# Attention scores in four PSUM banks instead of six, with one row maximum per two pairs of tokens

## The chip, the cores and the metric

The kernel runs on the 8 cores of one Trainium2 chip. Every core runs the same program on its own 2048 of the 16384 tokens, and no data passes between cores. The metric is the device time in microseconds of the slowest core, so lower is better.

## The reference

One layer in the form `x + attention(xn) + ffn(xn)`, where `xn` is the layer norm of `x` (1 x 16384 x 4096).

```python
q = einsum('bse,edh->bsdh', xn, Wq) + bq          # D = 128, 32 heads
k, v = (the same with 8 heads), then repeated 4 times
scores = einsum('bsdh,bseh->bsde', q, k) / sqrt(D)  # 128 x 128 for each token
attn = softmax(scores, axis=-1)
out = einsum('bsde,bseh->bsdh', attn, v)
...
base = einsum('bsi,oi->bso', xn, W)                # W from 4-bit weights, scale and zero
lora = einsum(einsum(xn, lora_A), lora_B) * 2
return x + out + base + lora
```

What is unusual is the attention. It doesn't run over positions: for each token by itself the 128 channels of q meet the 128 channels of k, with the heads as the contracted dimension. So there are 2048 score matrices of 128 x 128 on each core, each contracted over 8 head groups (the kernel has summed the four q heads that share a k head) or, with one more row for the maximum, over 9.

## The kernel before, in words

A core works through its 2048 tokens in 4 chunks of 512. A chunk has four stages, and the program writes them one behind the other on every engine, so each engine's queue has the same order:

1. The layer norm and its transposes into `xnT` (lines 285 to 380).
2. The projections for q, k and v (`qkv_t`, the matmuls of line 460) with weights that stream through the ring `wring`, and the small LoRA product (line 535).
3. The attention, in 16 batches of 32 tokens. A batch has 16 pairs of tokens. This is the stage that the change touches.
4. The FFN in 8 blocks of 512 columns (line 880), whose 4-bit weights VectorE (lines 830 and 833) and ScalarE (line 852) unpack just ahead of the matmuls.

A batch of the attention goes through these steps, each with its line:

- `_shf_half` (line 578): 16 small DMAs, 8 issued by SyncE and 8 by ScalarE, bring 32 tokens of q and k into `qg_sh` and `k_sh`, with heads on partitions. They wait until the B matmuls of the batch before are done.
- `att_A` (line 609): TensorE makes the scores of each pair (two matmuls of 128 columns, so 256 columns of f32 in PSUM), only so that a maximum can be taken.
- `att_rm` (line 626): VectorE takes the maximum of each row of each of the two score matrices, into two columns of `Mb`. There is one instruction per pair, 16 in a batch.
- `att_mt`, `att_mte`, `att_md` (lines 637, 648, 660): the maxima are transposed on TensorE, copied to SBUF and moved by one DMA into row 8 of `qg_sh`.
- `att_BAV` (lines 683 and 700): TensorE makes the scores again, transposed and with the maximum subtracted by the ninth contracted row (B), ScalarE takes the exponential (line 725), and TensorE multiplies the result with v (AV). On TensorE the order is B of pair 0, B of pair 1, AV of pair 0, B of pair 2, AV of pair 1, and so on.
- `att_rc` and `att_og` (lines 735 and 751): VectorE divides by the sum of the row.

Where scores lie in PSUM is said by `att_pp_aps`. A PSUM bank holds 512 columns of f32, hence two pairs. Six banks are used in turn: `pf0`, `pf1` and the four banks of `pAB`. Pair number `pp` takes bank `pp % 6`, and each second time round the other half of the bank. The waits go by bank and not by half:

```python
if pin >= 6:
    e.wait_ge(sem["rm"].h, rm_prev + pin - 5)
elif b > 0 or c > 0:
    e.wait_ge(sem["exp"].h, exp_prev + pin - 5)
```

In words, the A matmuls of pair `pin` wait until the maximum of pair `pin - 6` is taken. In the same way B of a pair waits for the exponential of the pair 6 before it. The stages around also use these banks: `pf0`, `pf1` and the first two banks of `pAB` hold the four results of 128 tokens in the projections and in the FFN.

Of the kernel before, what the change touches and what calls it, by code (L numbers as in the profile page):

```python
# [66 lines left out]
def build_program():  # L67
# [20 lines left out]
    with ExitStack() as ctx:  # L88
# [18 lines left out]
        Mb = sb("Mb", [128, 2 * 32], BF16)  # L107
# [31 lines left out]
        pf0 = psum("pf0", [128, 512], F32)  # L139
        pf1 = psum("pf1", [128, 512], F32)  # L140
        pAB = psum("pAB", [128, 2048], F32)
# [6 lines left out]
        sem = {n: S(nc, ctx, "s_" + n) for n in names}  # L148
# [127 lines left out]
        for c in range(min(NCH, KCHUNKS)):  # L276
# [273 lines left out]
            evq_ce = sem["evq"].v  # L550
            e7_vchan = sem["e7"].v

            def att_pp_aps(pp):
                sl = pp % 12
                bk = sl % 6
                hf = sl // 6
                if bk == 0:
                    t, off = pf0, hf * 256
                elif bk == 1:
                    t, off = pf1, hf * 256  # L560
                else:
                    t, off = pAB, (bk - 2) * 512 + hf * 256
                dsts = [t[:, off + j * 128: off + (j + 1) * 128] for j in range(2)]
                src = t.ap().rearrange("p (k x) -> p k x", x=128)[:, off // 128: off // 128 + 2, :]
                return dsts, src

            for b in (range(min(NBAT, KBATCH)) if KPHASE >= 3 else []):
                mblk = b // 4

# [19 lines left out]
                def att_A(e, c=c, b=b, rm_cb=rm_cb, exp_cb=exp_cb, evq_ce=evq_ce):  # L589
                    if KSTAGE < 1:  # L590
                        return
                    e.wait_ge(sem["shf"].h, sem["shf"].v)
                    if b == 0:
                        e.wait_ge(sem["evq"].h, evq_ce)
                        e.wait_ge(sem["evl"].h, sem["evl"].v)
                        e.wait_ge(sem["exp"].h, sem["exp"].v)
                    exp_prev = sem["exp"].v
                    rm_prev = sem["rm"].v
                    for pin in range(16):
                        pp = b * 16 + pin  # L600
                        dsts, _ = att_pp_aps(pp)
                        if pin >= 6:
                            e.wait_ge(sem["rm"].h, rm_prev + pin - 5)
                        elif b > 0 or c > 0:
                            e.wait_ge(sem["exp"].h, exp_prev + pin - 5)
                        last = None
                        for j in range(2):
                            slot = 2 * pin + j
                            last = e.matmul(dsts[j],  # L609
                                            qg_sh[0:8, slot * 128:(slot + 1) * 128],  # L610
                                            k_sh[0:8, slot * 128:(slot + 1) * 128],
                                            start=True, stop=True,
                                            skip_group_check=(j == 1))
                        sem["A"].inc(last)
                blk.tensor(att_A)

                def att_rm(e, b=b):
                    if KSTAGE < 2:
                        return
                    if sem["mdma"].v >= 32:  # L620
                        e.wait_ge(sem["mdma"].h, sem["mdma"].v - 16)
                    for pin in range(16):
                        e.wait_ge(sem["A"].h, sem["A"].v - 16 + pin + 1)
                        _, src = att_pp_aps(b * 16 + pin)
                        dstm = Mb[:, (b % 2) * 32 + 2 * pin: (b % 2) * 32 + 2 * pin + 2]
                        i = e.reduce_max(dstm, src, axis=AX.X, negate=True)  # L626
                        sem["rm"].inc(i)
                blk.vector(att_rm)

                t7b = sem["t7"].v  # L630
# [33 lines left out]
                def att_BAV(e, b=b, exp_cb=exp_cb, c=c, e7_vchan=e7_vchan):  # L664
                    if KSTAGE < 5:
                        return
                    e.wait_ge(sem["mdma"].h, sem["mdma"].v)
                    if b == 0:
                        e.wait_ge(sem["e7"].h, e7_vchan)
                    exp_start = sem["exp"].v  # L670
                    t0 = b * 32

                    def emit_B(pin):
                        pp = b * 16 + pin
                        dsts, _ = att_pp_aps(pp)
                        e.wait_ge(sem["rm"].h, sem["rm"].v - 16 + pin + 1)
                        need_ex = exp_start + pin - 5
                        if need_ex > 0:
                            e.wait_ge(sem["exp"].h, need_ex)
                        last = None  # L680
                        for j in range(2):
                            slot = 2 * pin + j
                            last = e.matmul(dsts[j],  # L683
                                            k_sh[0:9, slot * 128:(slot + 1) * 128],
                                            qg_sh[0:9, slot * 128:(slot + 1) * 128],
                                            start=True, stop=True,
                                            skip_group_check=True)
                        sem["B"].inc(last)

                    def emit_AV(pin):  # L690
                        if KSTAGE < 7:
                            return
                        e.wait_ge(sem["exp"].h, exp_start + pin + 1)
                        for j in range(2):
                            spos = 2 * pin + j
                            tok = t0 + spos
                            eslot = 2 * ((b * 16 + pin) % 4) + j
                            if spos == 0:
                                e.wait_ge(sem["ogs"].h, sem["ogs"].v)
                            ins = e.matmul(pV[:, spos * 9:spos * 9 + 9],  # L700
                                           Et[:, eslot * 128:(eslot + 1) * 128],
                                           v_chan[:, tok:tok + 8 * 512 + 1:512],
                                           start=(spos == 0), stop=(spos == 31))
                            sem["AV"].inc(ins)

                    for pin in range(16):
                        emit_B(pin)
                        if pin >= 1:
                            emit_AV(pin - 1)
                    emit_AV(15)  # L710
                blk.tensor(att_BAV)

                def att_exp(e, b=b, av_cb=av_cb):
                    if KSTAGE < 6:
                        return
                    for pin in range(16):
                        pp = b * 16 + pin
                        e.wait_ge(sem["B"].h, sem["B"].v - 16 + pin + 1)
                        need_av = av_cb + 2 * pp - 6
                        if need_av > 0:  # L720
                            e.wait_ge(sem["AV"].h, need_av)
                        _, src = att_pp_aps(pp)
                        eslot = 2 * (pp % 4)
                        dst = Et.ap().rearrange("p (s d) -> p s d", d=128)[:, eslot:eslot + 2, :]
                        i2 = e.activation(dst, src, AF.Exp, scale=INVSQ)  # L725
                        sem["exp"].inc(i2)
                blk.scalar(att_exp)

                def att_rc(e, b=b, ogs_cb=ogs_cb):
# [53 lines left out]
            for nb in (range(FNB) if KPHASE >= 4 else []):  # L783
# [80 lines left out]
                for half in range(2):  # L864
                    for m in range(MT):
                        def ffn_tmh(e, c=c, nb=nb, half=half, m=m, u0=u0,
                                    dqc0=dqc0, evq_ce=evq_ce, fui=fui):
                            if nb == 0 and half == 0 and m == 0:
                                e.wait_ge(sem["evq"].h, evq_ce)
                                e.wait_ge(sem["exp"].h, sem["exp"].v)  # L870
                            if half == 0 and fui >= 1:
                                e.wait_ge(sem["vt2"].h, 2 * (4 * (fui - 1) + m) + 1)
# [147 lines left out]
```

## Time and profile before

| what | value |
|---|---|
| time, median of 2 runs | 6877.63 us (6769.39 and 6985.87) |
| profiled execution, its own time | 6769.94 us |
| its span, slowest core (core 2) | 6768.2 us |
| spans of the 8 cores | 6730.1 to 6768.2 us |
| busy: TensorE matmul, VectorE, ScalarE | 3745.6, 1350.8, 1230.0 us |

The span runs from the first to the last instruction of the slowest core; the profiled execution's own time is 1.7 us longer than its span. Engines are PE (TensorE matmul), PEld (its weight load), DVE (VectorE), ACT (ScalarE), POOL (GpSimd) and SP (SyncE). A "q" behind a name is the engine's queue that issues DMAs. L609 is line 609 of the kernel. The share of busy time is a mean over four very different stages, so what follows reads the attention stage by itself.

### The profile page before, as it was taken

The numbers are of one execution on the slowest core, as the hardware profiler recorded it, in microseconds if no ns is written. First come the engines' busy times: TensorE is split into PE (matmuls) and PEld (weight loads), VectorE is DVE, ScalarE is ACT, GpSimd is POOL, SyncE is SP. The second block draws the span as 40 slices with busy tenths as digits, with TensorE's granted clock in tenths as the row PEclk, the third lists the DMA queues.
The fourth block names the chain that finished last, engine by engine and source line by source line (L and its number), as shares of the span: only waits on it lengthen the run. The fifth ranks groups of instructions, "written<-read, shape, count | busy, mean of one in ns | idle before, by whom it ended". The sixth has DMA issues, their size and how long they took to land.

```text
span 6768.2 us, 53961 instructions; the slowest of 8 cores (6730.1 to 6768.2 us)
## 1 busy us (share of the span) xinstructions
PE 3745.6 (55%) x17600; PEld 1620.1 (24%) x17600; DVE 1350.8 (20%) x2259; ACT 1230.0 (18%) x1664; POOL 272.6 (4%) x518
## 2 busy tenths in 40 slices
PE   0566644556266664456526666446562666544655
PEld 0222222212122222222112222222221222222222
DVE  3000122233300012222330001222323000222233
ACT  2000022222300002222230001222223000123222
POOL 0000000000000000000000000000000000000000
PEclk9878755667578875567658886556775888655767
DMA  2566400222212210023222221002222222100232
GB/s 72 136 169 163 126 6 6 74 103 95 91 68 88 91 56 6 6 79 111 97 80 75 87 88 49 6 6 103 92 97 75 87 87 88 37 6 11 105 107 80
DMA packets 146717, 508.58 MB, mean 75 GB/s; under 512 B 68100, under 2 KB 68308, under 8 KB 97302
## 3 DMA queue, kind: packets, MB, share of 16 engines
q0 software_dynamic: 62128, 378.23, 17.6%
q1 hardware_dynamic: 52840, 72.35, 3.1%
q10 hardware_dynamic: 31488, 54.56, 2.2%
q8 instruction: 159, 2.61, 0.2%
q14 instruction: 102, 0.84, 0.0%
HBM read 458.34 MB, written 84.03 MB: 80 GB/s over the span
## 4 chain that ended last, share of the span: by engine, by line
PE 44%; DMA 19%; DVE 13%; ACT 11%; issue 9%; ACTq 4%; DVEq 0%; SPq 0%; POOLq 0%; POOL 0%
PE pf L460 13%; PE pAB L460 9%; PE pAB L880 6%; PE pf L880 6%; ACT wring L852 5%; DMA wring<-wbq 4%; ACTq L578 4%; DVE Mb L626 3%; ACT Et L725 3%; PE pV L700 2%; DMA wring<-wq 2%; DMA qtb<-qt 2%; PE pAB L683 2%; DVE dqs L833 2%; DMA qg_sh<-Mt_s 2%
## 5 line engine op out<-in xcount | busy, mean ns | idle before, releaser
L460 PE MATMUL pf<-wring,xnT 128*128 128x512 bf16 x3072 | 873.8, 455 | 714.5 <-DMA wring<-wbq 326.3
L880 PE MATMUL pf<-wring,xnT 128*128 128x512 bf16 x2048 | 714.0, 511 | 507.6 <-ACT wring L852 507.6
L725 ACT ACT_TABLE_LOAD x64 | 82.1, 1283 | 3383.6 <-PE pf L683 2742.9
L460 PE MATMUL pAB<-wring,xnT 128*128 128x512 bf16 x3072 | 678.7, 379 | 0.0
L460 PEld LDWEIGHTS pf<-wring,xnT 128*128 128x128 bf16 x3072 | 339.7, 113 | 1246.8 <-issue 1019.6
L852 ACT ACTIVATE wring<-dqs 128x2048 bf16<-128x2048 int32 x256 | 488.8, 1909 | 585.5 <-DVE dqs L830 261.6
L880 PEld LDWEIGHTS pf<-wring,xnT 128*128 128x128 bf16 x2048 | 228.3, 119 | 987.6 <-issue 900.4
L880 PE MATMUL pAB<-wring,xnT 128*128 128x512 bf16 x2048 | 452.5, 379 | 0.0
L460 PEld LDWEIGHTS pAB<-wring,xnT 128*128 128x128 bf16 x3072 | 300.6, 98 | 362.4
L700 PE MATMUL pV<-v_chan,Et 128*128 128x9 bf16 x2048 | 216.6, 180 | 221.8 <-ACT Et L725 215.2
L609 PE MATMUL pAB<-k_sh,qg_sh 8*128 8x128 bf16 x1360 | 202.6, 290 | 225.7 <-DMA k_sh<-k_rm 224.5
L366 PE MATMUL pT<-identb,xns 128*128 128x128 bf16 x512 | 64.7, 306 | 455.8 <-ACT xns L349 410.1
L683 PE MATMUL pAB<-qg_sh,k_sh 9*128 9x128 bf16 x1360 | 246.1, 285 | 121.4 <-DMA qg_sh<-Mt_s 108.3
L493 DVE CAST qg_rm<-pf 128x512 bf16<-128x512 f32 x16 | 10.3, 686 | 1513.5 <-PE pf L471 1513.5
L725 ACT ACTIVATE Et<-pAB 128x256 bf16<-128x256 f32 x680 | 256.2, 384 | 175.4 <-PE pV L700 139.4
L626 DVE TENSOR_REDUCE Mb<-pAB 128x2 bf16<-128x256 f32 x680 | 241.1, 413 | 200.3 <-PE pAB L609 200.3
L880 PEld LDWEIGHTS pAB<-wring,xnT 128*128 128x128 bf16 x2048 | 200.5, 98 | 241.5
L830 DVE TENSOR_SCALAR dqs<-qtb 128x2048 int32<-128x2048 int32 x128 | 156.8, 1225 | 465.2 <-ACT wring L852 246.5
L700 PEld LDWEIGHTS pV<-v_chan,Et 128*128 128x128 bf16 x2048 | 137.2, 106 | 434.5 <-issue 434.4
L833 DVE TENSOR_SCALAR dqs<-qtb 128x2048 int32<-128x2048 int32 x128 | 157.1, 1227 | 315.1 <-ACT wring L852 253.8
L806 POOL DMA_DIRECT2D qtb<-qt x128 | 68.5, 536 | 3608.0 <-DVE dqs L833 3582.2
L735 DVE RECIPROCAL rz<-pV 128x32 f32<-128x32 f32 x64 | 22.9, 357 | 942.7 <-PE pV L700 942.7
(101 smaller groups left out, 2246.3 us busy)
## 6 DMA issues: line engine op xcount, KB each, us to landing
qtb<-qt POOLq DMA_DIRECT2D x128, 1024.0 KB, 5.1
wring<-wbq POOLq DMA_DIRECT2D x96, 1024.0 KB, 6.6
wring<-wq POOLq DMA_DIRECT2D x32, 1024.0 KB, 9.0
xt<-xin SPq DMA_DIRECT2D x16, 2048.0 KB, 8.0
wbq<-wring ACTq DMA_DIRECT2D x32, 1024.0 KB, 5.0
xr<-xin POOLq DMA_DIRECT2D x128, 256.0 KB, 5.9
out<-cmbU SPq DMA_DIRECT2D x128, 256.0 KB, 2.0
wring<-wbk POOLq DMA_DIRECT2D x24, 1024.0 KB, 6.6
```

Source lines behind the costliest of these rows:

```text
L460: ins = e.matmul(banks[m], xnT_ap(k, m), wring[:, slot * 512:(slot + 1) * 512], start=(jj == 0 and half == 0 and k == half * 16), stop=False)
L578: e.dma_start(out=dstv, in_=srcv).then_inc(sem["shf"].h, 16)
L609: last = e.matmul(dsts[j], qg_sh[0:8, slot * 128:(slot + 1) * 128], k_sh[0:8, slot * 128:(slot + 1) * 128], start=True, stop=True, skip_gr ...
L626: i = e.reduce_max(dstm, src, axis=AX.X, negate=True)
L683: last = e.matmul(dsts[j], k_sh[0:9, slot * 128:(slot + 1) * 128], qg_sh[0:9, slot * 128:(slot + 1) * 128], start=True, stop=True, skip_gr ...
L700: ins = e.matmul(pV[:, spos * 9:spos * 9 + 9], Et[:, eslot * 128:(eslot + 1) * 128], v_chan[:, tok:tok + 8 * 512 + 1:512], start=(spos == ...
L725: i2 = e.activation(dst, src, AF.Exp, scale=INVSQ)
L806: e.dma_start(out=qtb[:, (h % 2) * 2048:(h % 2 + 1) * 2048], in_=src).then_inc(sem["qtl"].h, 16)
L830: i = e.tensor_scalar(dqs[:], srcq, 4, None, ALU.logical_shift_right)
L833: i = e.tensor_scalar(dqs[:], srcq, 15, None, ALU.bitwise_and)
L852: i = e.activation(wring[:, s0 * 512:(s0 + 4) * 512], dqs[:], AF.Identity)
L880: ins = e.matmul(banks4[m], xnT_ap(k, m), wring[:, slot * 512:(slot + 1) * 512], start=(k == 0), stop=(k == 31))
```

## The change

Four things are done.

- The ring of score banks has four banks instead of six, all in `pAB`. Pair `pp` takes bank `pp % 4`, and each second time round the other half. A of a pair from the fifth on waits for the maximum that covers the pair 4 before it, and B waits for the exponential of the pair 4 before it.
- VectorE takes the maxima of two pairs with one instruction, which reads 256 columns in each of two neighbouring banks and writes four columns of `Mb`. There are 8 such instructions in a batch, and each waits for A of both its pairs.
- The waits on the maxima (`rm`) are counted in these new units, so two pairs of A wait for the same count.
- In the FFN the wait for all exponentials (`exp`) stands ahead of the third group of matmuls (`m == 2`, which writes `pAB`) and not ahead of the first (`m == 0`, which writes `pf0`).

```diff
                     for pin in range(16):
                         pp = b * 16 + pin
-                        dsts, _ = att_pp_aps(pp)
-                        if pin >= 6:
-                            e.wait_ge(sem["rm"].h, rm_prev + pin - 5)
+                        sl = pp % 8
+                        bcol = (sl % 4) * 512 + (sl // 4) * 256
+                        if pin >= 4:
+                            e.wait_ge(sem["rm"].h, rm_prev + (pin - 4) // 2 + 1)
                         elif b > 0 or c > 0:
-                            e.wait_ge(sem["exp"].h, exp_prev + pin - 5)
+                            e.wait_ge(sem["exp"].h, exp_prev + pin - 3)
                         last = None
                         for j in range(2):
                             slot = 2 * pin + j
-                            last = e.matmul(dsts[j],
+                            last = e.matmul(pAB[:, bcol + j * 128:bcol + (j + 1) * 128],
...
-                    for pin in range(16):
-                        e.wait_ge(sem["A"].h, sem["A"].v - 16 + pin + 1)
-                        _, src = att_pp_aps(b * 16 + pin)
-                        dstm = Mb[:, (b % 2) * 32 + 2 * pin: (b % 2) * 32 + 2 * pin + 2]
+                    for pj in range(8):
+                        e.wait_ge(sem["A"].h, sem["A"].v - 16 + 2 * pj + 2)
+                        sl = (b * 16 + 2 * pj) % 8
+                        a0 = ((sl % 4) * 512 + (sl // 4) * 256) // 256
+                        src = pAB.ap().rearrange("p (a j x) -> p a j x", j=2, x=128)[:, a0:a0 + 3:2, :, :]
+                        dstm = Mb[:, (b % 2) * 32 + 4 * pj: (b % 2) * 32 + 4 * pj + 4].rearrange(
+                            "p (a j) -> p a j", j=2)
                         i = e.reduce_max(dstm, src, axis=AX.X, negate=True)
                         sem["rm"].inc(i)
...
-                        e.wait_ge(sem["rm"].h, sem["rm"].v - 16 + pin + 1)
-                        need_ex = exp_start + pin - 5
+                        sl = pp % 8
+                        bcol = (sl % 4) * 512 + (sl // 4) * 256
+                        e.wait_ge(sem["rm"].h, sem["rm"].v - 8 + pin // 2 + 1)
+                        need_ex = exp_start + pin - 3
...
                             if nb == 0 and half == 0 and m == 0:
                                 e.wait_ge(sem["evq"].h, evq_ce)
+                            if nb == 0 and half == 0 and m == 2:
                                 e.wait_ge(sem["exp"].h, sem["exp"].v)
```

On TensorE, the A matmuls of the first batch stood like this before. A row is a line of the kernel, the operation, what it writes and reads, its size, the semaphores that it waits for, and how many such instructions follow one another. `s_rm` counts the maxima:

```order
L609 MATMUL pf<-k_sh,qg_sh 128x128 [waits s_shf,s_evq,s_evl,s_exp]
L609 MATMUL pf<-k_sh,qg_sh 128x128 x3
L609 MATMUL pAB<-k_sh,qg_sh 128x128 x8
L609 MATMUL pf<-k_sh,qg_sh 128x128 [waits s_rm]
L609 MATMUL pf<-k_sh,qg_sh 128x128
L609 MATMUL pf<-k_sh,qg_sh 128x128 [waits s_rm]
```

and they stand like this now:

```order
L596 MATMUL pAB<-k_sh,qg_sh 128x128 [waits s_shf,s_evq,s_evl,s_exp]
L596 MATMUL pAB<-k_sh,qg_sh 128x128 x7
L596 MATMUL pAB<-k_sh,qg_sh 128x128 [waits s_rm]
L596 MATMUL pAB<-k_sh,qg_sh 128x128
L596 MATMUL pAB<-k_sh,qg_sh 128x128 [waits s_rm]
```

The first wait on a maximum stood behind 12 matmuls (six pairs) and stands behind 8 (four pairs).

On VectorE, the maxima of a later batch and what follows them stood like this before:

```order
L626 TENSOR_REDUCE Mb<-pAB 128x2 [waits s_A] x2
L626 TENSOR_REDUCE Mb<-pf 128x2 [waits s_A] x2
L626 TENSOR_REDUCE Mb<-pAB 128x2 [waits s_A] x4
L626 TENSOR_REDUCE Mb<-pf 128x2 [waits s_A] x2
L626 TENSOR_REDUCE Mb<-pAB 128x2 [waits s_A] x4
L626 TENSOR_REDUCE Mb<-pf 128x2 [waits s_A] x2
L651 UNCONDITIONAL_BRANCH
L648 COPY Mt_s<-pT 32x128 [waits s_t7]
```

and they stand like this now:

```order
L616 TENSOR_REDUCE Mb<-pAB 128x4 [waits s_A] x8
L641 UNCONDITIONAL_BRANCH
L638 COPY Mt_s<-pT 32x128 [waits s_t7]
L731 UNCONDITIONAL_BRANCH
L728 RECIPROCAL rz<-pV 128x32 [waits s_AV]
```

Sixteen instructions of two columns each have become eight of four columns.

On TensorE, at the end of a chunk's attention, the last AV matmuls, the transposes of the result and the first FFN matmuls stood like this before:

```order
L700 MATMUL pV<-v_chan,Et 128x9 [waits s_exp]
L700 MATMUL pV<-v_chan,Et 128x9
L770 UNCONDITIONAL_BRANCH
L766 MATMUL pT<-identb,og 128x128 [waits s_ogs,s_e7]
L766 MATMUL pT<-identb,og 128x128 x7
L889 UNCONDITIONAL_BRANCH
L880 MATMUL pf<-wring,xnT 128x512 [waits s_evq,s_exp,s_dqc]
```

and they stand like this now:

```order
L691 MATMUL pV<-v_chan,Et 128x9 [waits s_exp]
L691 MATMUL pV<-v_chan,Et 128x9
L763 UNCONDITIONAL_BRANCH
L759 MATMUL pT<-identb,og 128x128 [waits s_ogs,s_e7]
L759 MATMUL pT<-identb,og 128x128 x7
L883 UNCONDITIONAL_BRANCH
L874 MATMUL pf<-wring,xnT 128x512 [waits s_evq,s_dqc]
```

The wait on `s_exp` has left the first FFN matmul; the matmuls ahead of it, which wait on `s_exp` themselves, stand where they stood.

## Rows read from the trace of the kernel before

**Rows 1.** The page: the span, and busy tenths in 40 equal slices.
```profile
span 6768.2 us, 53961 instructions; the slowest of 8 cores (6730.1 to 6768.2 us)
...
PE   0566644556266664456526666446562666544655
...
DVE  3000122233300012222330001222323000222233
...
PEclk9878755667578875567658886556775888655767
DMA  2566400222212210023222221002222222100232
```

**Rows 2.** Busy time by stretch: the attention stages of the four chunks.
```profile
core 2: us, PE busy (x) PEld busy (x) DVE busy (x) ACT busy (x) POOL busy (x), PEclk, DMA share, GB/s
808.00:1238.00 430.00, 210.83 (x1569) 113.03 (x1569) 103.43 (x305) 115.99 (x270) 0.00 (x0) 0.50 0.03 6
2474.00:2904.00 430.00, 209.27 (x1553) 111.91 (x1550) 103.42 (x305) 114.67 (x266) 0.00 (x0) 0.50 0.03 6
4139.00:4569.00 430.00, 209.46 (x1546) 111.75 (x1544) 104.09 (x306) 112.53 (x261) 0.00 (x0) 0.51 0.03 6
5804.00:6244.00 440.00, 219.79 (x1605) 116.28 (x1603) 104.14 (x307) 116.84 (x272) 0.00 (x0) 0.51 0.03 6
```

**Rows 3.** Chain that ended last, one batch: start us, us, what.
```profile
862.70 1.01 PE pAB L609 x8
863.71 0.43 PE pf L609 x4
864.14 0.65 PE pAB L609 x6
864.84 0.32 DVE Mb L626
...
867.16 1.42 DVE Mb L626 x4
869.59 1.76 DMA qg_sh<-Mt_s
```

**Rows 4.** Timeline of VectorE in the same batch: start us, us, instructions merged.
```profile
863.18 1.42 DVE L626 TENSOR_REDUCE Mb<-pAB 128x2 bf16<-128x256 f32 x4 [5.44 <-PE pAB L609]
...
866.50 0.74 DVE L626 TENSOR_REDUCE Mb<-pf 128x2 bf16<-128x256 f32 x2
867.16 1.40 DVE L626 TENSOR_REDUCE Mb<-pAB 128x2 bf16<-128x256 f32 x4
```

**Rows 5.** Timeline of TensorE in the same batch.
```profile
862.70 1.01 PE L609 MATMUL pAB<-k_sh,qg_sh 8*128 8x128 bf16 x8 [5.97 <-DMA k_sh<-k_rm]
863.51 0.63 PE L609 MATMUL pf<-k_sh,qg_sh 8*128 8x128 bf16 x4
863.93 1.17 PE L609 MATMUL pAB<-k_sh,qg_sh 8*128 8x128 bf16 x8
865.07 0.70 PE L609 MATMUL pf<-k_sh,qg_sh 8*128 8x128 bf16 x4
868.82 0.26 PE L637 MATMUL pT<-identb,Mb 128*32 128x128 bf16 x1 [1.73 <-DVE Mb L626]
```

**Rows 6.** Timeline of VectorE, 864.6 to 864.8 us: the batch's fifth maximum.
```profile
864.51 0.41 DVE L626 TENSOR_REDUCE Mb<-pf 128x2 bf16<-128x256 f32 x1
```

**Rows 7.** Lines 609 and 493, one instruction: min/median/max ns.
```profile
L609 PE MATMUL pAB<-k_sh,qg_sh x1360: 211/306/309, 808.3 to 6226.7; 8*128 8x128 bf16 x195
...
L493 DVE CAST qg_rm<-pAB x16: 678/680/682, 388.4 to 5611.0; 128x512 bf16<-128x512 f32 x16
```

**Rows 8.** Timeline of VectorE, 380 to 390 us: reads of 512 PSUM columns.
```profile
387.21 1.29 DVE L493 CAST qg_rm<-pf 128x512 bf16<-128x512 f32 x2 [193.84 <-PE pf L471]
388.42 1.28 DVE L493 CAST qg_rm<-pAB 128x512 bf16<-128x512 f32 x2
```

**Rows 9.** Groups by line: exponentials, maxima, and two sizes of reduction: busy us, mean ns.
```profile
L725 ACT ACTIVATE Et<-pAB 128x256 bf16<-128x256 f32 x680 | 256.2, 384 | 175.4 <-PE pV L700 139.4 <-PE pAB L683 8.6
...
L626 DVE TENSOR_REDUCE Mb<-pAB 128x2 bf16<-128x256 f32 x680 | 241.1, 413 | 200.3 <-PE pAB L609 200.3
...
L309 DVE TENSOR_REDUCE ss<-xt 128x1 f32<-128x4096 f32 x16 | 70.7, 4419 | 40.9 <-DMA xt<-xin 40.7
...
L312 DVE TENSOR_REDUCE ss<-sq 128x1 f32<-128x2048 f32 x16 | 36.4, 2276 | 0.0
```

**Rows 10.** Timeline of ScalarE in the same batch: the exponentials.
```profile
874.88 0.86 ACT L725 ACTIVATE Et<-pAB 128x256 bf16<-128x256 f32 x2 [0.72 <-PE pV L700]
876.16 0.86 ACT L725 ACTIVATE Et<-pf 128x256 bf16<-128x256 f32 x2 [0.42 <-PE pV L700]
```

**Rows 11.** Timeline of TensorE, end of the first chunk's attention.
```profile
1239.22 0.20 PE L700 MATMUL pV<-v_chan,Et 128*128 128x9 bf16 x2 [0.28 <-ACT Et L725]
1240.75 1.01 PE L766 MATMUL pT<-identb,og 128*128 128x128 bf16 x8 [1.32 <-DVE og L751]
1247.30 1.87 PE L880 MATMUL pf<-wring,xnT 128*128 128x512 bf16 x4 [5.54 <-ACT wring L852]
```

More of the change, by code:

```diff
@@ L551, in build_program @@
             e7_vchan = sem["e7"].v
[L553 to L565, printed above, removed]
             for b in (range(min(NBAT, KBATCH)) if KPHASE >= 3 else []):
@@ L674, in emit_B @@
                         pp = b * 16 + pin
-                        dsts, _ = att_pp_aps(pp)
-                        e.wait_ge(sem["rm"].h, sem["rm"].v - 16 + pin + 1)
-                        need_ex = exp_start + pin - 5
+                        sl = pp % 8
+                        bcol = (sl % 4) * 512 + (sl // 4) * 256
+                        e.wait_ge(sem["rm"].h, sem["rm"].v - 8 + pin // 2 + 1)
+                        need_ex = exp_start + pin - 3
                         if need_ex > 0:
@@ L682, in emit_B @@
                             slot = 2 * pin + j
-                            last = e.matmul(dsts[j],
+                            last = e.matmul(pAB[:, bcol + j * 128:bcol + (j + 1) * 128],
                                             k_sh[0:9, slot * 128:(slot + 1) * 128],
@@ L721, in att_exp @@
                             e.wait_ge(sem["AV"].h, need_av)
-                        _, src = att_pp_aps(pp)
+                        sl = pp % 8
+                        bk = ((sl % 4) * 512 + (sl // 4) * 256) // 128
+                        src = pAB.ap().rearrange("p (k x) -> p k x", x=128)[:, bk:bk + 2, :]
                         eslot = 2 * (pp % 4)
```

## The prediction

> **What bounds the kernel now.** I read the page first, for the shape of the run: four times over, a stretch with DMA near zero and TensorE's granted clock at 5 to 6 tenths [rows 1]. These are the attention stages. Busy time by stretch then says what each is: about 430 us long, with TensorE busy for 210, VectorE for 104 and ScalarE for 115 us [rows 2]. No engine is near full, so the stage is bound by a chain and not by throughput. The granted clock is 0.50 to 0.51, the lower of the two levels (1.2 GHz). The chain of one batch shows where the change acts [rows 3]. From the first A matmul at 862.70 us it runs through A matmuls and then through maxima on VectorE, and ends with four maxima in a row at 867.16 + 1.42 = 868.58 us. Only then come the transpose on TensorE at 868.82 us, which waited for the maxima [rows 5], and the DMA of the maxima [rows 3]. So this phase, from the first A matmul to the last maximum, is on the path in full. By the timeline it takes 867.16 + 1.40 - 862.70 = 5.86 us [rows 4, 5]. I call it the maximum phase. There are 64 of them (4 chunks of 16 batches), 375 us in all, and nothing else of the core's work runs under them. Every 1 us per batch is worth 64 us, and 2% of the run (about what a measurement of this kernel can tell from no change) is 135 us, or 2.1 us per batch.
>
> **Who sets the pace in the maximum phase now.** VectorE does. Two maxima take 0.74 us and one takes 0.41 us, so one starts 0.33 us after another; the four at 863.18 us say the same, (1.42 - 0.41) / 3 = 0.34 [rows 4, 6]. Sixteen in a row make 15 x 0.33 + 0.41 = 5.4 us, and the first starts 0.48 us behind the first matmul. TensorE is faster: two matmuls of a pair need 0.21 us, since four matmuls take 0.63 us of which 0.31 is the last one's own length, hence 0.107 us each [rows 5, 7]. TensorE runs six pairs ahead and is then released by the maxima. The price of a release can be read off: the fifth maximum ends at 864.51 + 0.41 = 864.92 us [rows 6], and the matmul that waited for it starts at 865.07 us [rows 5], 0.15 us later. Its pair's own maximum isn't taken before 866.50 us [rows 4], when the pair has been ready for about 1 us. The ring of six hides release and refill; VectorE never waits inside a batch.
>
> **The change part by part.**
>
> *The fused maximum.* How long does VectorE take over 512 columns of PSUM instead of 256? No row shows this reduction, so I bound it. A reduction of 4096 elements takes 4419 ns and one of 2048 takes 2276 ns, so 256 more elements cost 2143 / 8 = 268 ns [rows 9], and 413 + 268 = 0.68 us. The casts of 512 columns out of PSUM are the nearest rows in width: one is 0.68 us long [rows 7] and two take 1.28 us, so they start 0.60 us apart [rows 8]. I take 0.68 us long and 0.60 us apart. The upper bound is that fusing saves nothing: 2 x 0.41 = 0.82 us long and 0.74 apart. The lower bound is 0.60 us long as well. If VectorE stayed the pace, 8 x 0.60 against 16 x 0.33 would save 0.5 us per batch.
>
> The Trainium skill, page "VectorE: DVE Perf Modes", section "The TRN2 errata — SBUF-src ops pay a fixed extra latency per instruction", gives a VectorE instruction that reads PSUM a cost of 120 cycles plus one per column at 0.96 GHz. It would make the fused maximum 0.66 us long, and by it alone each fusing saves 0.125 us. The rows agree for the length (413 ns, where it gives 392) and not for the pace, where starting 0.60 instead of 2 x 0.33 us apart saves 0.06.
>
> *The ring of four with release by twos.* This is what counts. Now the first maximum needs two pairs: 0.48 + 2 x 0.107 = 0.69 us behind the first matmul. Number the fused maxima g0 to g7. The pairs of g2 lie in the banks of g0, so they can't start before g0 has ended. From the start of g0 to the start of g2 there are: 0.68 us for g0 itself, 0.15 us until TensorE starts, and 0.69 us for four matmuls and the hand-over to VectorE. The sum is 1.52 us. In between VectorE does g1, for which it needs 0.60, and is then idle for 1.52 - 1.20 = 0.32 us. So a cycle of two fused maxima (four pairs) takes 1.52 us, where four single ones took 4 x 0.33 = 1.33 us. The odd ones follow the even ones by 0.60, both on VectorE and by their own release (TensorE is idle again by then: its four matmuls occupy it for 0.43 us).
>
> The phase is 0.69 (start of g0) + 3 x 1.52 (start of g6) + 0.60 (start of g7) + 0.68 (its length) = 6.53 us. Against 5.86 that is 0.67 us more, on the path in full, times 64 = 43 us. With the bounds of the fused maximum: at 0.82 long and 0.74 apart the cycle is 1.66 and the phase 0.69 + 4.98 + 0.74 + 0.82 = 7.23 us, 88 us more; at 0.60 long the cycle is 1.44 and the phase 6.21 us, 22 us more.
>
> The Trainium skill, page "Perfetto Trace Analysis", section "Matmul Optimizations", says to use all eight PSUM banks so that instructions can overlap. It speaks against this edit, and the sum above is what it costs by the rows of this kernel.
>
> *The B half of the batch.* B of a pair now waits for the exponential 4 before it instead of 6. On TensorE's queue B of pair n stands behind AV of pair n - 2, which itself waits for the exponential of pair n - 2, so both waits are long met. The rows show the loop's pace: two exponentials every 1.28 us (874.88 to 876.16), each pair of them behind AV work [rows 10]. A ring of four is still two more than this order uses. Cost 0. If that cover were gone, each pair would cost up to one exponential more (the third rival). The count of maxima that B waits for is complete before the DMA of the maxima, so it costs 0 as well.
>
> *The FFN wait.* The first FFN matmul stands behind all AV matmuls on TensorE, and the last of these waits for the last exponential. In the trace it starts at 1247.30 us, 8 us after the last AV, and waited for line 852, the unpacking on ScalarE [rows 11]. Moving the wait gains 0.
>
> *DMAs.* None is added or moved past another. The 16 small DMAs still wait for B, and they come 0.67 us later with all that follows.
>
> **Sum.** 6769.9 us (the profiled execution) + 43 = 6813 us, 0.6% slower and less than can be told. The median shown, 6877.6, lies 1.6% above the profiled execution, as the midpoint of two runs 3.2% apart. The same 43 us on it would give 6921, and the range reaches there.
>
> **Rivals.**
>
> - *VectorE stays fed* (not slower). Then the phase is 0.69 + 7 x 0.60 + 0.68 = 5.57 us, 0.29 less, times 64 = 19 us less: 6751 us. It decides at the hand-over between the engines: release and refill must take no more than 1.20 - 0.68 = 0.52 us, where the rows give 0.15 + 0.69 = 0.84. Even if VectorE could start after one pair, 0.15 + 0.48 would be over 0.52. For it: the 0.15 is read off at one place, and a release might overlap with the length of the fused maximum. Chance 0.08. By the Trainium skill's charge per instruction (the page on VectorE and section named above), eight charges fewer save 8 x 0.125 = 1 us per batch, an estimate of 6706 us if only VectorE counted; the maxima's pace in the trace bears out half of that at most.
> - *The two-bank read costs as much as two reads*: 6858 us, worked out above. For it: no row shows a read across banks. Against it: the other wide reads cost by the column. Chance 0.10.
> - *The B half falls to the pace of the ring.* If B really had to wait out one exponential per pair, 16 x 0.384 = 6.1 us per batch would be added [rows 9], 393 us in all and 7160 us; a third of that, 2.1 us per batch, is where it turns into a difference that can be told. It needs the order on TensorE to be other than AV behind B, which it isn't. Chance 0.03.
> - *The freed banks let the FFN start early.* At most the 8 us between last AV and first FFN matmul, four times, so 32 us off the forecast: 6781 us. Against it, that gap ends with ScalarE's unpacking. Chance 0.03.
>
> **How the numbers follow.** The forecast has the remaining 0.76, with a range of its own from 6785 to 6835 for its inputs. Faster by over 2% would need 135 us, more than VectorE's whole saving: 0.02. Slower by over 2% has the third rival and an unseen effect of the clock: 0.04. Within 2%: 0.94. The range of 6745 to 6925 takes in the first, second and fourth rival, and above them the gap between the two runs shown.
>
> **What would show it.** In the changed profile: line 616 has 512 instructions of about 680 ns. In a batch VectorE starts them alternately 0.60 and 0.92 us apart, with VectorE idle for 0.92 - 0.68 = 0.24 us ahead of every even one. The first A matmul is some 6.5 us ahead of the last maximum's end. The exponentials keep their 1.28 us per two, and the attention stages are each 10 to 11 us longer, with projections and FFN as before. The forecast is wrong if the maxima come evenly 0.60 us apart (then the first rival holds), if each takes 0.8 us (then the second), or if the stages outside the attention change their length.

## The result and the profile after

| what | before | after |
|---|---|---|
| median, all runs | 6797.6 us (42 runs) | 6817.24 us (43 runs) |
| profiled execution's span, slowest core | 6768.2 us | 6806.8 us |
| ratio of the changed kernel to before | | 1.0054, 95% interval 1.0032 to 1.0076 |

The change makes the kernel 0.5% slower, clear of noise. Some executions of either kernel have a lower granted clock on the cores of one die and take longer; the ratio leaves these out and the medians don't, so the two medians lie only 20 us apart (0.3%). The median of 6817 us stands beside a forecast of 6813 us. The two executions known ahead of the forecast had a median of 6877.63 us; with 42 it is 6797.6 us. The profiled executions took 6769.94 us before and 6808.51 us after, 38.6 us apart.

The page of the changed kernel has the same shape in 40 slices as before, and nearly the same busy time on each engine [rows 1]. From these lines alone one wouldn't find the change:

```profile
span 6806.8 us, 52725 instructions; the slowest of 8 cores (6777.4 to 6806.8 us)
...
PE   0566644556256664455526666445562666544655
...
DVE  3000122232300012223330001222323000122233
...
PEclk9878755677578875567758886556775778655767
```

The timelines of one batch show it. VectorE first, to be read against [rows 4]:

```profile
864.83 1.29 DVE L616 TENSOR_REDUCE Mb<-pAB 128x4 bf16<-128x512 f32 x2 [5.65 <-PE pAB L596]
866.35 1.29 DVE L616 TENSOR_REDUCE Mb<-pAB 128x4 bf16<-128x512 f32 x2 [0.24 <-PE pAB L596]
867.87 1.29 DVE L616 TENSOR_REDUCE Mb<-pAB 128x4 bf16<-128x512 f32 x2 [0.23 <-PE pAB L596]
869.40 1.29 DVE L616 TENSOR_REDUCE Mb<-pAB 128x4 bf16<-128x512 f32 x2 [0.23 <-PE pAB L596]
```

and TensorE in the same batch, to be read against [rows 5]:

```profile
864.14 1.01 PE L596 MATMUL pAB<-k_sh,qg_sh 8*128 8x128 bf16 x8 [5.96 <-DMA k_sh<-k_rm]
865.67 1.18 PE L596 MATMUL pAB<-k_sh,qg_sh 8*128 8x128 bf16 x8 [0.52 <-DVE Mb L616]
867.19 1.18 PE L596 MATMUL pAB<-k_sh,qg_sh 8*128 8x128 bf16 x8 [0.34 <-DVE Mb L616]
868.71 1.18 PE L596 MATMUL pAB<-k_sh,qg_sh 8*128 8x128 bf16 x8 [0.34 <-DVE Mb L616]
870.94 0.26 PE L627 MATMUL pT<-identb,Mb 128*32 128x128 bf16 x1 [1.05 <-DVE Mb L616]
```

The two engines now take turns. VectorE does two fused maxima in 1.29 us and then waits 0.24 us for TensorE; TensorE makes four pairs and then waits 0.34 us for VectorE. Before, VectorE had no idle row inside a batch. One cycle is 866.35 to 867.87, so 1.52 us for four pairs. The phase from the first A matmul to the end of the last maximum is 869.40 + 1.29 - 864.14 = 6.55 us, where it was 5.86.

The groups by line add this up for the whole run, of the changed kernel (busy us, mean ns | idle us before them, and its releaser):

```profile
L616 DVE TENSOR_REDUCE Mb<-pAB 128x4 bf16<-128x512 f32 x512 | 331.4, 687 | 365.9 <-PE pAB L596 364.4
...
L718 ACT ACTIVATE Et<-pAB 128x256 bf16<-128x256 f32 x1024 | 384.2, 383 | 262.5 <-PE pV L691 205.3
```

The 512 maxima of 687 ns are what was forecast (0.68 us). The exponentials cost what they did [rows 9]. The idle time ahead of the maxima has 16 x 4 x 3 = 192 gaps inside batches in it, most of them of 0.23 to 0.24 us. Added up over the trace they make 43 us that weren't there before.

The phases of all 64 batches, added up over each trace, make 374.8 us before and 418.6 us after, 43.8 us more. On core 0 of both traces the four attention stages (each from the first A matmul to the last AV) make 1728.6 and 1775.1 us, so 11.6 us more each, where 10 to 11 was forecast. The rest of that core's span is 5033.0 us before and 5031.7 us after, so outside the attention nothing changed its length.

### The profile page after: what moved, and what is told of

Same layout as the page of the kernel before. It is cut to its first block, busy times and chain, and to the rows that moved or that the text cites. A ratio compares the mean times of both kernels' runs of the same rounds, so it can differ in the third digit from the quotient of the medians.

```text
span 6806.8 us, 52725 instructions; the slowest of 8 cores (6777.4 to 6806.8 us)
## 1 busy us (share of the span) xinstructions
PE 3729.8 (55%) x17384; PEld 1631.2 (24%) x17600; DVE 1336.9 (20%) x1747; ACT 1229.0 (18%) x1664; POOL 272.6 (4%) x518
## 4 chain that ended last, share of the span: by engine, by line
PE 41%; DMA 20%; DVE 13%; ACT 11%; issue 10%; ACTq 4%; DVEq 1%; SPq 0%; POOLq 0%; POOL 0%
PE pf L460 13%; PE pAB L460 9%; PE pAB L874 5%; PE pf L874 5%; ACT wring L845 5%; DMA wring<-wbq 4%; ACTq L564 4%; DMA qtb<-qt 4%; DVE Mb L616 3%; PE pAB L674 3%; ACT Et L718 3%; PE pV L691 2%; DMA wring<-wq 2%; PE pAB L596 2%; DVE dqs L826 2%
## 5 line engine op out<-in xcount | busy, mean ns | idle before, releaser
L460 PE MATMUL pf<-wring,xnT 128*128 128x512 bf16 x3008 | 869.9, 457 | 717.4 <-DMA wring<-wbq 323.0
L874 PE MATMUL pf<-wring,xnT 128*128 128x512 bf16 x2004 | 700.1, 509 | 516.6 <-ACT wring L845 514.6
L596 PE MATMUL pAB<-k_sh,qg_sh 8*128 8x128 bf16 x2048 | 283.6, 293 | 429.2 <-DMA k_sh<-k_rm 340.6
L674 PE MATMUL pAB<-qg_sh,k_sh 9*128 9x128 bf16 x2048 | 370.6, 285 | 190.7 <-DMA qg_sh<-Mt_s 171.3
L718 ACT ACTIVATE Et<-pAB 128x256 bf16<-128x256 f32 x1024 | 384.2, 383 | 262.5 <-PE pV L691 205.3
L616 DVE TENSOR_REDUCE Mb<-pAB 128x4 bf16<-128x512 f32 x512 | 331.4, 687 | 365.9 <-PE pAB L596 364.4
L596 PEld LDWEIGHTS pAB<-k_sh,qg_sh 8*128 8x128 bf16 x2048 | 175.7, 115 | 529.8 <-issue 527.5
```

Source lines behind the costliest of these rows:

```text
L460: ins = e.matmul(banks[m], xnT_ap(k, m), wring[:, slot * 512:(slot + 1) * 512], start=(jj == 0 and half == 0 and k == half * 16), stop=False)
L596: last = e.matmul(pAB[:, bcol + j * 128:bcol + (j + 1) * 128], qg_sh[0:8, slot * 128:(slot + 1) * 128], k_sh[0:8, slot * 128:(slot + 1) * ...
L674: last = e.matmul(pAB[:, bcol + j * 128:bcol + (j + 1) * 128], k_sh[0:9, slot * 128:(slot + 1) * 128], qg_sh[0:9, slot * 128:(slot + 1) * ...
L874: ins = e.matmul(banks4[m], xnT_ap(k, m), wring[:, slot * 512:(slot + 1) * 512], start=(k == 0), stop=(k == 31))
```

## The experiments

All compare with the kernel before on the same chip. Where a ratio is given, its interval is a 95% one. The time given is the median of all executions. Beside it I read one batch in each profile, since most batches have the same phase: within 0.02 us of the median in 60 of 64 before and in 46 of 64 in the changed kernel (where the others are from 5.98 to 6.92 us).

**A ring of four, maxima one by one.** The kernel before, with four banks and all else kept:

```diff
-                sl = pp % 12
-                bk = sl % 6
-                hf = sl // 6
...
+                sl = pp % 8
+                t, off = pAB, (sl % 4) * 512 + (sl // 4) * 256
...
-                        if pin >= 6:
-                            e.wait_ge(sem["rm"].h, rm_prev + pin - 5)
+                        if pin >= 4:
+                            e.wait_ge(sem["rm"].h, rm_prev + pin - 3)
...
-                        need_ex = exp_start + pin - 5
+                        need_ex = exp_start + pin - 3
```

> The kernel before with a ring of four banks in pAB and still one maximum per pair, released pair by pair. Theory (the cost comes from the release by twos on a short ring): a single release needs 0.41 + 0.15 + 0.48 = 1.04 us from the start of one maximum to the start of the one four pairs later, VectorE needs 4 x 0.33 = 1.32 us for these, so VectorE stays busy, the maximum phase stays 5.86 us and the time is that of before (ratio 1.000, within 0.2%). Rival (a ring of four banks costs by itself, in the A or the B half): the phase is 6.2 us or more, or AV and B take longer than 12.2 us per batch, and the ratio is 1.004 or more.

Measured: ratio 0.9966 (0.9928 to 1.0004), 6768.52 us. VectorE in one batch of this kernel, and then TensorE:

```profile
861.90 5.39 DVE L619 TENSOR_REDUCE Mb<-pAB 128x2 bf16<-128x256 f32 x16 [5.44 <-PE pAB L602]
...
861.43 5.05 PE L602 MATMUL pAB<-k_sh,qg_sh 8*128 8x128 bf16 x32 [5.97 <-DMA k_sh<-k_rm]
```

Sixteen maxima in one row of 5.39 us, which is 15 x 0.33 + 0.41, so there is no idle time between them. 861.90 + 5.39 - 861.43 = 5.86 us is the phase of before. From the first B matmul to the last AV a batch takes 12.21 us at the median of the 64, and 12.20 us in the kernel before. Two banks fewer cost nothing as long as each maximum releases its own pair. The rival falls in both halves.

**Six banks, fused maxima.** The kernel before with its six banks laid out as one tensor `pS`, and the fused maximum of the change:

```diff
-        pf0 = psum("pf0", [128, 512], F32)
-        pf1 = psum("pf1", [128, 512], F32)
-        pAB = psum("pAB", [128, 2048], F32)
+        pS = psum("pS", [128, 3072], F32)
+        pf0 = pS[:, 0:512]
+        pf1 = pS[:, 512:1024]
+        pAB = pS[:, 1024:3072]
...
-                            e.wait_ge(sem["rm"].h, rm_prev + pin - 5)
+                            e.wait_ge(sem["rm"].h, rm_prev + (pin - 6) // 2 + 1)
...
+                        sl = (b * 16 + 2 * pj) % 12
+                        a0 = (sl % 6) * 2 + sl // 6
+                        src = pS.ap().rearrange("p (a j x) -> p a j x", j=2, x=128)[:, a0:a0 + 3:2, :, :]
```

> The kernel before with its six banks (as one PSUM tensor) and fused maxima of two pairs. Theory: three groups of two pairs are in flight, a release cycle of 0.69 + 0.15 + 0.69 = 1.53 us stands against 3 x 0.60 = 1.80 us of VectorE, so VectorE stays busy and the phase is 0.69 + 7 x 0.60 + 0.69 = 5.58 us, 0.28 less than before: 18 us less, ratio 0.997. Rival (the fused maximum as such is the cost): the phase stays near 6.5 us and the ratio near 1.005.

Measured: ratio 0.9955 (0.9916 to 0.9995), 6750.34 us. VectorE in one batch, and TensorE:

```profile
855.70 4.87 DVE L625 TENSOR_REDUCE Mb<-pS 128x4 bf16<-128x512 f32 x8 [5.47 <-PE pS L605]
...
855.01 4.49 PE L605 MATMUL pS<-k_sh,qg_sh 8*128 8x128 bf16 x32 [5.78 <-DMA k_sh<-k_rm]
```

Eight in one row of 4.87 us, about 7 x 0.60 + 0.68, so without a gap: the phase is 855.70 + 4.87 - 855.01 = 5.56 us. So fusing by itself gains 0.30 us per batch. The cost is neither in the fusing nor in the ring, but in both together.

**Four banks, the two pairs of a maximum in one bank.** The changed kernel with another layout in the A half. TensorE fills a bank with two pairs and VectorE reads that bank, so four groups fit where there were two. The first pair of a batch now waits for all exponentials of the batch before; its wait still ends with the DMA of `k_sh` (the row of TensorE below), as before [rows 5]:

```diff
-                        bcol = (sl % 4) * 512 + (sl // 4) * 256
-                        if pin >= 4:
-                            e.wait_ge(sem["rm"].h, rm_prev + (pin - 4) // 2 + 1)
-                        elif b > 0 or c > 0:
-                            e.wait_ge(sem["exp"].h, exp_prev + pin - 3)
+                        bcol = (pin % 8) * 256
+                        if pin >= 8:
+                            e.wait_ge(sem["rm"].h, rm_prev + (pin - 8) // 2 + 1)
+                        elif pin == 0 and (b > 0 or c > 0):
+                            e.wait_ge(sem["exp"].h, exp_prev)
...
-                        a0 = ((sl % 4) * 512 + (sl // 4) * 256) // 256
+                        a0 = (2 * pj) % 8
-                        src = pAB.ap().rearrange("p (a j x) -> p a j x", j=2, x=128)[:, a0:a0 + 3:2, :, :]
+                        src = pAB.ap().rearrange("p (a j x) -> p a j x", j=2, x=128)[:, a0:a0 + 2, :, :]
```

> The changed kernel with the same four banks and the same fused maxima, but the two pairs of one maximum share a bank in the A half, so that four groups are in flight instead of two. Theory: a release cycle of 1.53 us stands against 4 x 0.60 = 2.4 us, the phase is 5.58 us, ratio to before 0.997. Rival (the number of banks sets it): the phase stays at 6.5 us, ratio 1.005. Whether a maximum over one bank is shorter than one over two is seen beside it: 0.69 us if not.

Measured: ratio 0.9966 (0.9927 to 1.0006), 6773.97 us. VectorE in one batch, TensorE, and then the min, median and max of VectorE's line in ns:

```profile
848.15 4.87 DVE L613 TENSOR_REDUCE Mb<-pAB 128x4 bf16<-128x512 f32 x8 [5.64 <-PE pAB L594]
...
847.46 3.89 PE L594 MATMUL pAB<-k_sh,qg_sh 8*128 8x128 bf16 x32 [5.96 <-DMA k_sh<-k_rm]
...
L613 DVE TENSOR_REDUCE Mb<-pAB x512: 677/678/692, 794.3 to 6192.5; 128x4 bf16<-128x512 f32 x171
```

The phase is 848.15 + 4.87 - 847.46 = 5.56 us again, with the four banks of the change. What counts is how many groups are in flight, not how many banks there are. A maximum over one bank takes 678 ns at the median. Over two banks, in the kernel with six banks, where VectorE is never idle either, eight took the same 4.87 us: reading across banks costs nothing.

**The FFN wait put back.** The changed kernel with `m == 0` in place of `m == 2`:

```diff
-                            if nb == 0 and half == 0 and m == 2:
+                            if nb == 0 and half == 0 and m == 0:
                                 e.wait_ge(sem["exp"].h, sem["exp"].v)
```

> The changed kernel with the wait for the exponentials back ahead of the first FFN matmul. Theory: no difference to the changed kernel, ratio to before 1.005, first FFN matmul still about 8 us behind the last AV. Rival (the moved wait gives something back): slower than the changed kernel by up to 8 us for each of 4 chunks, ratio 1.010.

Measured: ratio 1.004 (0.9995 to 1.0084), 6854.68 us. The rival's 1.010 lies outside the interval, and the changed kernel's 1.0054 inside. The weight loads at the end of an attention stage are the sharper reading (a few matmul records are missing there in the changed kernel's trace, its weight loads aren't). The changed kernel, second chunk:

```profile
2932.99 0.14 PEld L691 LDWEIGHTS pV<-v_chan,Et 128*128 128x128 bf16 x2 [0.37 <-issue]
2934.51 0.77 PEld L759 LDWEIGHTS pT<-identb,og 128*128 128x128 bf16 x8 [1.39 <-issue]
2941.00 0.14 PEld L874 LDWEIGHTS pf<-wring,xnT 128*128 128x128 bf16 x2 [5.72 <-issue]
```

and with the wait back, first chunk:

```profile
1244.78 0.14 PEld L691 LDWEIGHTS pV<-v_chan,Et 128*128 128x128 bf16 x2 [0.49 <-issue]
...
1252.86 0.14 PEld L874 LDWEIGHTS pf<-wring,xnT 128*128 128x128 bf16 x2 [5.77 <-issue]
```

By these rows it is 8.01 us from the last AV to the FFN in the second chunk of the one and 8.08 us in the first chunk of the other. That is a difference between chunks and not between kernels: the four chunks take 8.07, 8.02, 8.02 and 8.02 us in the kernel before, in the changed one and with the wait back. Moving the wait does nothing.

**A ring of two, maxima one by one.** This goes to the point where the sum says that even single maxima must starve, and where a B half paced by its ring would have to show:

```diff
-                sl = pp % 12
...
+                sl = pp % 4
+                t, off = pAB, (sl % 2) * 512 + (sl // 2) * 256
...
-                        if pin >= 6:
-                            e.wait_ge(sem["rm"].h, rm_prev + pin - 5)
+                        if pin >= 2:
+                            e.wait_ge(sem["rm"].h, rm_prev + pin - 1)
...
-                        need_ex = exp_start + pin - 5
+                        need_ex = exp_start + pin - 1
```

> The kernel before with a ring of only two banks, in both halves of a batch, and one maximum per pair. Theory: in the A half the release cycle of two pairs, 0.41 + 0.15 + 0.48 = 1.04 us, is over the 0.66 us of VectorE, so the phase is 0.47 + 7 x 1.04 + 0.33 + 0.41 = 8.5 us instead of 5.86 (169 us more, 2.5%). In the B half the ring costs nothing, since on TensorE B already stands behind AV of the pair two before it: B and AV stay at 12.2 us per batch. Rival (the B half is paced by its ring too): B and AV take over 13 us per batch.

Measured, one run: 6981.2 us, beside a median of 6784.5 us for the kernel before. TensorE's first A matmuls of one batch, and VectorE's maxima, of which there are eight rows that are alike:

```profile
871.36 0.58 PE L602 MATMUL pAB<-k_sh,qg_sh 8*128 8x128 bf16 x4 [5.96 <-DMA k_sh<-k_rm]
...
871.84 0.76 DVE L619 TENSOR_REDUCE Mb<-pAB 128x2 bf16<-128x256 f32 x2 [5.43 <-PE pAB L602]
872.88 0.76 DVE L619 TENSOR_REDUCE Mb<-pAB 128x2 bf16<-128x256 f32 x2 [0.29 <-PE pAB L602]
873.92 0.76 DVE L619 TENSOR_REDUCE Mb<-pAB 128x2 bf16<-128x256 f32 x2 [0.28 <-PE pAB L602]
...
879.14 0.76 DVE L619 TENSOR_REDUCE Mb<-pAB 128x2 bf16<-128x256 f32 x2 [0.29 <-PE pAB L602]
```

The cycle is 1.04 us for two pairs, to the hundredth what the sum gives, and the phase is 879.14 + 0.76 - 871.36 = 8.54 us. Over the 64 batches the phases make 547.1 us, 172 us more than before, where 169 was worked out. The run as a whole is 197 us over the median of before. What is left isn't in the phases: outside the attention stages core 0 of this one execution took 47 us more than in the kernel before, and core 5 no more. Why is open. ScalarE in the same batch:

```profile
887.52 0.86 ACT L718 ACTIVATE Et<-pAB 128x256 bf16<-128x256 f32 x2 [0.45 <-PE pV L693]
888.80 0.90 ACT L718 ACTIVATE Et<-pAB 128x256 bf16<-128x256 f32 x2 [0.42 <-PE pV L693]
890.08 0.90 ACT L718 ACTIVATE Et<-pAB 128x256 bf16<-128x256 f32 x2 [0.38 <-PE pV L693]
```

Two exponentials every 1.28 us, exactly as with six banks [rows 10]. From the first B to the last AV a batch takes 12.20 us at the median. So the B half doesn't feel its ring even at two banks, and the rival falls: the order on TensorE, with AV of pair n - 2 ahead of B of pair n, is the tighter bond.

**One maximum over four pairs.** The kernel with two pairs in a bank, with a fused maximum of 1024 columns. Two groups are in flight again, so the same sum can be tried at another size. B of a batch now waits for all its maxima at once, which the DMA of the maxima makes it do anyway:

```diff
-                            e.wait_ge(sem["rm"].h, rm_prev + (pin - 8) // 2 + 1)
+                            e.wait_ge(sem["rm"].h, rm_prev + (pin - 8) // 4 + 1)
...
-                    for pj in range(8):
-                        e.wait_ge(sem["A"].h, sem["A"].v - 16 + 2 * pj + 2)
+                    for pj in range(4):
+                        e.wait_ge(sem["A"].h, sem["A"].v - 16 + 4 * pj + 4)
```

> Four banks as in the run with two pairs in a bank, but one maximum over four pairs (1024 columns, two banks), so that two groups are in flight. Theory, the same sum at another size: the maximum is 0.68 + 512 x 1.05 ns = 1.22 us long and 1.13 apart at best, the cycle 1.22 + 0.15 + 1.12 = 2.49 us against 2.26 of VectorE, and the phase 1.12 + 2.49 + 1.13 + 1.22 = 5.96 us (6 us over before in all). Rival (fewer instructions are always better when a bank is shared): under 5.56 us.

Measured, one run: 6769.14 us. VectorE in one batch, and TensorE in the same:

```profile
859.70 4.84 DVE L613 TENSOR_REDUCE Mb<-pAB 128x8 bf16<-128x1024 f32 x4 [6.07 <-PE pAB L594]
```

```profile
858.58 1.86 PE L594 MATMUL pAB<-k_sh,qg_sh 8*128 8x128 bf16 x16 [5.96 <-DMA k_sh<-k_rm]
861.07 2.13 PE L594 MATMUL pAB<-k_sh,qg_sh 8*128 8x128 bf16 x16 [0.62 <-DVE Mb L613]
```

The phase is 859.70 + 4.84 - 858.58 = 5.96 us, as worked out. A quarter of the instructions of before, and yet 0.1 us longer: the first fill takes 1.12 us, and TensorE waits 0.62 us for a release. (VectorE's gap is too short here for the timeline to part the row. One run can't tell its time from the 6784.5 us of before; the phase is what it shows.)

**The first two pairs by themselves.** Two pairs in a bank, but the first two maxima of a batch single, each pair in its own bank. Here too B waits for all maxima at once:

```diff
+                        g = pin // 2
+                        bcol = pin * 512 if g == 0 else ((g + 1) % 4) * 512 + (pin % 2) * 256
+                        if g >= 3:
+                            e.wait_ge(sem["rm"].h, rm_prev + g - 2)
...
+                    for pin in range(2):
+                        e.wait_ge(sem["A"].h, sem["A"].v - 16 + pin + 1)
...
-                    for pj in range(8):
+                    for pj in range(1, 8):
```

> Two pairs in a bank and fused maxima as before, but the first two pairs of a batch with a maximum each, so that VectorE starts after one pair. Theory: 0.47 + 0.33 + 0.33 + 6 x 0.60 + 0.68 = 5.41 us instead of 5.56, 9 to 10 us less than that kernel in all and 28 us less than before: ratio to before 0.996. Rival (the first fill isn't on the path): 5.56 us, 0.997.

Measured: 6742.4 us, ratio 0.9947 (0.9916 to 0.9979). VectorE in one batch, and TensorE:

```profile
859.37 0.76 DVE L612 TENSOR_REDUCE Mb<-pAB 128x2 bf16<-128x256 f32 x2 [5.26 <-PE pAB L595]
860.04 4.27 DVE L620 TENSOR_REDUCE Mb<-pAB 128x4 bf16<-128x512 f32 x7
...
858.90 3.75 PE L595 MATMUL pAB<-k_sh,qg_sh 8*128 8x128 bf16 x32 [5.79 <-DMA k_sh<-k_rm]
```

The phase is 860.04 + 4.27 - 858.90 = 5.41 us. This version is faster than before clear of noise, and faster than the changed kernel. That it beats the layout without single maxima shows in the phase (5.41 against 5.56 us); the two ratios, 0.9947 and 0.9966, can't be told apart.

The phases side by side, worked out ahead of each run and measured in one batch:

| kernel | groups in flight, pairs in each | phase expected, us | measured, us |
|---|---|---|---|
| before | 6, 1 | (read) | 5.86 |
| changed | 2, 2 | 6.53 | 6.55 |
| ring of four, single | 4, 1 | 5.86 | 5.86 |
| six banks, fused | 3, 2 | 5.58 | 5.56 |
| four banks, pairs in one bank | 4, 2 | 5.58 | 5.56 |
| ring of two, single | 2, 1 | 8.5 | 8.54 |
| one maximum over four pairs | 2, 4 | 5.96 | 5.96 |
| first two pairs single | 4, 1 and then 2 | 5.41 | 5.41 |

## Why the prediction was right or wrong

**The maximum phase as the place.** Right. It grew from 5.86 to 6.55 us, 0.69 us where 0.67 was forecast. Times 64 that is 44 us, which the sum over all batches bears out (43.8); the ratio of 1.0054 on the 6769.9 us of the profiled execution is 37 us, with an interval of 22 to 51.

**The fused maximum.** Right: 687 ns on average for 0.68 us. The upper bound of 0.82 us, that a read over two banks costs as two reads (the second rival), is refuted by these 687 ns, since each of these maxima reads two banks. The saving of fusing is there (0.30 us per batch in that run, with 0.29 worked out in the first rival). The change doesn't get it.

**The cycle of 1.52 us.** Right, to the hundredth, with 0.24 us of idle time on VectorE ahead of every even maximum, as named. Of the six runs with other depths and sizes, five came out within 0.02 us of the sum and the ring of two within 0.05 (8.54 for 8.49). So the three terms (the maximum's length, 0.15 us for the release, the fill up to the hand-over) are the cause and not only a sum that fits.

**The B half and the FFN wait at nothing.** Right, and both shown: by a ring of two that leaves the exponentials at 1.28 us for two, and by the wait put back. The third and the fourth rival fall with it.

**The number of banks.** The prediction sets its sum beside the advice to use all eight banks, as what it costs not to. The runs show that the number isn't what costs: with four banks the phase is 5.86 us with single maxima and 5.56 us with fused ones, where the two pairs of a maximum share a bank.

**The first rival.** Its condition, release and refill within 0.52 us, isn't met in the changed kernel; where it is made void by more groups in flight, its number comes true (5.56 us for the 5.57 that it gave).

**The size against what can be told.** This is the step that failed. The 43 us were right, and what the prediction made of them was not. It took 2% as what a measurement of this kernel can tell, called the 43 us "0.6% slower and less than can be told", and so gave its weight (0.94) to no difference. What the runs showed in its place: over 43 and 42 runs the comparison tells 0.22% to each side, and 1.0032 to 1.0076 leaves out 1. The change is slower, and not the same. The 2% fitted only the two runs shown at first, which lay 3.2% apart. The phase in the trace is the same in most batches, so 64 times 0.67 us could have been called a slowdown on its evidence.

The base of the sum belongs to the same step. The 43 us were added to the one profiled execution, 6769.9 us, and not to the median shown, 6877.63 us. Beside that median the forecast of 6813 us reads as 0.9% faster, while its text says slower. The profiled executions are the like pair, and they lie 38.6 us apart. That the median after, 6817 us, falls 4 us from the forecast is in part luck: 43 us on the median before, 6797.6 us, would be 6841.

The range of 6745 to 6925 us was for the same reason far wider than the terms. The narrower one of 6785 to 6835 has no working; the bounds that the prediction did work out for the fused maximum, 22 and 88 us, give 6792 to 6858.

## What to carry to other kernels

When two engines hand a ring of buffers to each other, write down the release cycle (length of the consumer's instruction, its release, the producer's fill for one group) and set it against the consumer's own pace times the groups in flight. Fusing two of the consumer's instructions saves a little of its time (here 0.06 us: 0.60 us for one fused maximum where two single ones take 2 x 0.33), but it also doubles the fill and halves the groups in flight, so fuse over buffers that can be released together (here two pairs in one bank) and keep the first group small. And when the waits go by bank, as here, count the ring in groups of banks that one instruction holds, not in slots.

## What the runs showed of the hardware that was not expected

- A maximum that follows another at once takes about 680 ns for 512 columns. In the changed kernel the even ones, which start after an idle time, take 690 to 692 ns and most of the odd ones 680 to 684 (687 ns on average), so starting from idle costs some 10 ns. With 256 columns the means are 413 ns [rows 9] and, in the run with a ring of two, 421 ns.
- The release of 0.15 us from the end of a maximum to the start of the matmul that waits for it is the same for maxima of 256 columns (864.92 to 865.07 us, [rows 5, 6]) and of 1024 (1.22 us long, so 859.70 + 1.22 = 860.92 to 861.07 us). In the changed kernel it is 145 to 147 ns in all 64 batches.
- VectorE reads across two banks at the same pace as within one: eight maxima take 4.87 us both ways (the runs with six banks, and with two pairs in one bank).
